# First layer's experts with tokens in rows: ScalarE applies the gates, GpSimd adds to the residual

## The chip, the cores and the metric

The kernel runs on one core of a Trainium2 chip. The metric is the device time of one execution in microseconds (us), lower is better. The core has five engines that run programs of their own and meet at semaphores: TensorE (PE; its weight loads are listed apart as PEld), VectorE (DVE), ScalarE (ACT), GpSimd (POOL) and SyncE (SP), which issues DMAs.

## The reference, cut to what matters

Two layers over 2048 tokens of width 128. Each has a mixing part (a selective scan in the first, attention in the second) and a part with experts. The change is in the experts of the first layer: a shared expert without a gate and eight gated ones, all of them computed for every token.

```python
def _L0_ffn_ref(x, shared_w1, shared_w2, experts_w1, experts_w2, gate_w):
    shared = jnp.einsum('td,dh->th', x_flat, shared_w1.T)
    shared = jnp.einsum('th,hd->td', jax.nn.silu(shared), shared_w2.T)
    gate_logits = x_flat @ gate_w.T
    top_k_gates, top_k_idx = jax.lax.top_k(gate_logits, TOP_K)
    top_k_gates = jax.nn.softmax(top_k_gates, axis=1)
    gates = gates.at[jnp.arange(T)[:, None], top_k_idx].set(top_k_gates)
    h = jnp.einsum('td,ehd->teh', x_flat, experts_w1)
    expert_out = jnp.einsum('teh,edh->ted', jax.nn.silu(h), experts_w2)
    selected = jnp.einsum('ted,te->td', expert_out, gates)
    return (shared + selected).reshape(B, S, D)
...
x = x + _L0_attn_ref(_layernorm(x, axis=-1), ...)
x = x + _L0_ffn_ref(_layernorm(x, axis=-1), ...)
```

Width 128, hidden width 512, eight experts, the two best are used.

## The kernel before

The tokens are cut into four chunks of 512 (`tc` 0 to 3). Every engine's program is written out in one shared order (`scan_order`): 64 steps `k` of the scan, 16 for each chunk. A step has a fixed sequence of calls, and a call does something only on the engines that define it. In step k DVE runs two halves of `scanP` (L1411), `mulW` (L1417) and `scanX` (L1425); POOL runs `mulB(k+1)` (L1876), `mulC(k)` (L1883) and `clamp(k+2)` (L1892); PE ends the step with `sums(k-1)` (L669); ACT opens it with two Exp (L1160), for step k+2. `mulB(k+1)` writes a ring of three buffers and waits for `sums(k-2)`; `mulW(k+1)` waits for `mulB(k+1)`.

Between these calls lie slots in which a generator is pulled: three slots of a step for the prolog of the next chunk, four for the epilog, gates and experts (`ffn`) of the chunk before. So the experts of chunk tc run beside the scan of chunk tc+1, one expert per step; those of chunk 3 run after the scan, beside the first parts of the second layer, and then begin the next part.

`ffn(tc)` has 36 pulls n, four for each of nine experts x (x = 0 is the shared one). In pull n PE multiplies by a quarter of the first weight ("up", L725) into bank 4 or 5; ACT applies Silu (L1187) and writes one of six buffers HB; two pulls later PE multiplies this by a quarter of the second weight ("down", L716), and four downs are summed in one bank. For chunks 0 to 2 there is only one bank for downs, 6: the first down of expert x+1 waits for the semaphore `gated`, which says that expert x has been read out. For chunk 3 two banks alternate. In pulls of one step, PE's order is: up, down; up, down; up; up, down, down; then the sums. The first down of the next expert is the one right behind the fourth up.

The result of the downs has features in rows (partitions) and tokens in columns. The gates have tokens in rows, so PE transposes them (L700), ACT copies them out (L1179), SP writes them to DRAM and reads each expert's row back to all partitions (buffers GB). DVE multiplies bank 6 by GB into GO (L1506), POOL adds GO to FO (L1904), and at the end PE transposes FO back ("fold", L739) and DVE adds it to the residual x_tok (L1520). Of the shared expert, ACT makes a plain copy into FO (L1191). While ACT computes Silu and Exp in turn, each change loads a table (ACT_TABLE_LOAD).

Of the kernel before, what the change touches and what calls it, by code (L numbers as in the profile page):

```python
# [384 lines left out]
def build(nc, A, out):  # L385
    with ExitStack() as ctx:
# [47 lines left out]
        with ExitStack() as ph:  # L434
# [37 lines left out]
            gT0 = sa("gT0", [8, C])  # L472
            gd = nc.dram_tensor("gd", [4, 8, C], F32, kind="Internal").ap()
            GB = [sa(f"GB{i}", [128, C])[:, :] for i in range(3)]
# [117 lines left out]
        def tensor_program(e):  # L592
# [79 lines left out]
            def epilog(tc):  # L672
# [3 lines left out]
                w.wait_ge(S("x_ffn"), tc)  # L676
# [19 lines left out]
            def gates(tc):  # L696
                yield from idle(9)
                w.wait_ge(S("gt"), 18 * tc + 18)
                for b in range(4):
                    t = e.transpose(bank(SUM_BANK[tc])[0:8, 128 * b:128 * b + 128], G[:, b, :], ident[:, :])  # L700
                t.then_inc(S("mm_gT"), 1)
                yield
                yield from idle(2)

            def down(i):

                tc, n = divmod(i, 36)
                w.wait_ge(S("hid"), i + 1)
                if n % 4 == 0:
                    if tc < 3:  # L710
                        w.wait_ge(S("gated"), 9 * tc + n // 4)
                    else:
                        w.wait_ge(S("gated"), 27 + max(n // 4 - 1, 0))
                        w.wait_ge(S("y"), 8)
                    w.wait_ge(S("g_row"), tc + 1)
                e.matmul(down_bank(tc, n // 4), f_w2[:, n // 4, n % 4, :], HB1[i % 6], start=(n % 4 == 0),  # L716
                         stop=(n % 4 == 3)).then_inc(S("mm_down"), 1)

            def ffn(tc):
# [14 lines left out]
                yield  # L734
                yield
# [5 lines left out]
                yield  # L741
                yield from idle(2)
# [78 lines left out]
            def qside(c):  # L821
# [4 lines left out]
                if c == 3:  # L826
                    w.wait_ge(S("x_ffn"), 4)
# [15 lines left out]
            def take_max(m):  # L843
                if m >= 2:
                    w.wait_ge(*freed(m - 2))
                else:
                    w.wait_ge(S("hid"), 144)
                    w.wait_ge(S("x_ffn"), 4)
# [489 lines left out]
        def vector_program(e):  # L1338
# [170 lines left out]
            def ffn(tc):  # L1509
                for n in range(36):  # L1510
                    if n % 4 == 2 and n >= 10:
                        gate_expert(tc, n // 4 - 1)
# [826 lines left out]
```

## Time and profile before

| | before |
|---|---|
| time, median of 3 runs | 1585.73 us (1584.5 to 1588.5) |
| profiled execution: own time, span | 1584.67 us, 1582.9 us |
| PE, DVE, ACT, POOL busy, share of the span | 83%, 79%, 66%, 42% |
| mean granted clock of TensorE | 0.906 of full speed |

A busy share is a mean over stages that have different limits. The scan takes up to about 625 us of the span, the experts of chunk 3 with the preparation of attention up to about 770 us, and attention and the second layer's experts the rest. The experts of the first layer run from 221 to 317 us, from 375 to 471 us, from 524 to 616 us, and from 643 to 767 us.

### The profile page before, as it was taken

To read this page: it belongs to the slowest core of one execution; us is meant where nothing else is said; L and a number is where in the kernel's file an instruction comes from. 1 tells how busy PE (TensorE), PEld (TensorE's weight loads), DVE (VectorE), ACT (ScalarE), POOL (GpSimd) and SP (SyncE) were. 2 spreads that over 40 slices of the span, in tenths; PEclk is the share of its full clock that TensorE was granted. 3 is DMA by queue.
4 is the path that set the end of the run, shared out by engine and by line. 5 is a ranking of instruction groups with operands and counts; after the bars stand their busy time and mean duration, and the time that the engine had idled before them with its cause. 6 is when DMAs were issued, how large, how long until landed. Compare 5 with 4: busy or idle time off the path is not lost.

```text
span 1582.9 us, 22572 instructions
## 1 busy us (share of the span) xinstructions
PE 1315.4 (83%) x8408; PEld 510.9 (32%) x8408; DVE 1250.9 (79%) x1499; ACT 1043.0 (66%) x1823; POOL 664.2 (42%) x609
## 2 busy tenths in 40 slices
PE   4355669966994797788749999999999999999998
PEld 1111233423342343333212222222222222225973
DVE  1889977888789888277579999999999999942522
ACT  3442357636862673545319999899989998998653
POOL 0678856875787586656232111311121114111440
PEclk9675589978997798899768999999999999999999
DMA  7122212312222220242121211000010000000210
GB/s 223 59 63 79 67 50 79 87 60 69 71 72 64 74 80 27 53 88 43 36 42 32 68 31 47 13 12 2 2 22 2 2 2 15 9 22 16 72 32 27
DMA packets 63696, 75.71 MB, mean 48 GB/s; under 512 B 8633, under 2 KB 39226, under 8 KB 63458
## 3 DMA queue, kind: packets, MB, share of 16 engines
q1 hardware_dynamic: 62818, 72.70, 17.0%
q0 software_dynamic: 768, 1.57, 0.3%
q8 instruction: 66, 1.08, 0.3%
q14 instruction: 44, 0.36, 0.1%
HBM read 66.04 MB, written 8.21 MB: 47 GB/s over the span
## 4 chain that ended last, share of the span: by engine, by line
PE 47%; DVE 29%; POOL 10%; issue 9%; ACT 4%; DMA 1%; SPq 1%; DVEq 0%; POOLq 0%; ACTq 0%
DVE mx L1636 15%; PE PS L945 11%; PE PS L933 6%; PE PS L716 4%; PE PS L902 4%; PE PS L725 4%; POOL D L1876 4%; DVE D L1425 3%; DVE PS L1411 3%; POOL D L1883 2%; PE PS L1017 2%; PE PS L1032 2%; PE PS L669 2%; DVE PS L1417 2%; PE PS L637 2%
## 5 line engine op out<-in xcount | busy, mean ns | idle before, releaser
L1297 ACT ACTIVATE aa<-PS 128x512 f32<-128x512 f32 x1024 | 551.6, 598 | 57.4 <-PE PS L933 46.6
L1636 DVE TENSOR_REDUCE mx<-PS 128x2 f32<-128x1024 f32 x480 | 552.2, 1216 | 8.0 <-PE PS L902 5.2
L945 PE MATMUL PS<-aa,D 128*32 128x256 f32 x4096 | 321.6, 391 | 1.5 <-ACT aa L1297 0.6
L933 PE MATMUL PS<-D 54*128 54x512 bf16 x1024 | 212.0, 390 | 9.3 <-ACT aa L1297 8.9
L669 PE MATMUL PS<-D,ident 128*128 128x512 f32 x256 | 157.5, 750 | 62.0 <-POOL D L1883 54.5
L902 PE MATMUL PS<-D 51*128 51x512 bf16 x960 | 189.9, 385 | 17.6 <-DVE mx L1636 17.0
L1990 POOL CAST n<-nm 4x512 bf16<-4x512 f32 x15 | 9.1, 604 | 445.9 <-ACT nm L1279 445.9
L1883 POOL TENSOR_TENSOR D<-D 128x1024 f32<-128x1024 f32 x64 | 150.8, 2356 | 72.6 <-DVE D L1425 72.6
L1160 ACT ACTIVATE D<-D,Am 128x512 f32<-128x512 f32 x128 | 85.1, 713 | 129.3 <-DVE D L1425 127.4
L1876 POOL TENSOR_TENSOR D<-D 128x1024 f32<-128x1024 f32 x64 | 150.5, 2352 | 41.1 <-PE PS L669 36.5
L1411 DVE TENSOR_TENSOR_SCAN PS<-PS,D 128x512 f32<-128x512 f32 x128 | 157.6, 1231 | 11.4 <-POOL D L1892 3.5
L725 PE MATMUL PS<-xnT,f_w 128*128 128x512 f32 x288 | 152.9, 631 | 6.0 <-ACT HB L1187 6.0
L1187 ACT ACTIVATE HB<-PS 128x512 f32<-128x512 f32 x144 | 85.1, 597 | 108.1 <-PE PS L725 107.7
L716 PE MATMUL PS<-HB,f_w 128*128 128x512 f32 x288 | 149.3, 626 | 0.9 <-ACT FO L1191 0.9
L945 PEld LDWEIGHTS PS<-aa,D 128*32 128x32 f32 x4096 | 84.2, 108 | 191.9 <-issue 153.0
L933 PEld LDWEIGHTS PS<-D 54*128 54x128 bf16 x1024 | 53.3, 93 | 219.6 <-ACT aa L1297 159.7
L1425 DVE TENSOR_TENSOR_SCAN D<-D,hl,PS 128x512 f32<-128x512 f32 x96 | 122.4, 1275 | 1.9
L669 PEld LDWEIGHTS PS<-D,ident 128*128 128x128 f32 x256 | 57.4, 237 | 145.0 <-POOL D L1883 73.5
L1417 DVE SCALAR_TENSOR_TENSOR PS<-PS,D 128x512 f32<-128x512 f32 x128 | 88.9, 694 | 3.5 <-POOL D L1876 0.5
L716 PEld LDWEIGHTS PS<-HB,f_w 128*128 128x128 f32 x288 | 57.2, 200 | 77.9 <-issue 70.5
L725 PEld LDWEIGHTS PS<-xnT,f_w 128*128 128x128 f32 x288 | 54.7, 200 | 72.7 <-issue 60.1
L598 PE MATMUL PS<-ident,xn 128*128 128x128 f32 x48 | 10.5, 358 | 79.8 <-ACT xn L1076 79.8
(323 smaller groups left out, 1634.4 us busy)
## 6 DMA issues: line engine op xcount, KB each, us to landing
D<-bc SPq DMA_DIRECT2D x128, 256.0 KB, 3.4
GB<-gd SPq DMA_DIRECT2D x32, 256.0 KB, 3.9
D<-sc SPq DMA_DIRECT2D x72, 64.0 KB
aa<-in_L_ffn_W SPq DMA_DIRECT2D x9, 256.0 KB, 3.2
D<-in_L_ffn_W SPq DMA_DIRECT2D x9, 256.0 KB, 3.7
f_w<-in_L_ffn_experts_w SPq DMA_DIRECT2D x1, 2048.0 KB, 9.6
f_w<-in_L_ffn_experts_w SPq DMA_DIRECT2D x8, 256.0 KB, 6.1
aa<-gh SPq DMA_DIRECT2D x1, 2048.0 KB, 9.3
```

Source lines behind the costliest of these rows:

```text
L669: e.matmul(bank(g), ident[:, :], wb[k % 3][:, g, :], start=(n == 0), stop=(n == 15)).then_inc(S("mm_sum"), 1)
L716: e.matmul(down_bank(tc, n // 4), f_w2[:, n // 4, n % 4, :], HB1[i % 6], start=(n % 4 == 0), stop=(n % 4 == 3)).then_inc(S("mm_down"), 1)
L725: e.matmul(bank(4 + i % 2), f_w1[:, n // 4, 128 * (n % 4):128 * (n % 4) + 128], XN[:, ts], start=True, stop=True).then_inc(S("mm_up"), 1)
L902: t = e.matmul(to[:, hh, :], query(hh, qc % 2, p, b), KS[64 * hh:64 * hh + 51, p, 512 * c:512 * c + 512], start=True, stop=True)
L933: e.matmul(take_exp(s + hh), KS[64 * hh:64 * hh + 54, p, 128 * kb:128 * kb + 128], QP[64 * hh:64 * hh + 54, qc % 2, p, :], start=True, sto ...
L945: t = e.matmul(PS[32 * j:32 * j + 32, 7, cs], va[:, kb, 9 * h:9 * h + 32], Pt[K % 3][:, 512 * j + 256 * n:512 * j + 256 * n + 256], start= ...
L1297: e.activation(Pt[K % 3][:, c:c + 512], bank((s + hh) % 3), ACT.Exp).then_inc(S("e_free"), 1)
L1411: e.tensor_tensor_scan(out=bank(3), data0=bank(2), data1=ab[k % 3][:, g, :], initial=0.0, op0=ALU.max, op1=ALU.mult).then_inc(S("sP"), 1)
L1425: e.tensor_tensor_scan(out=pb[k % 2][:, g, :], data0=ab[k % 3][:, g, :], data1=bank(3), initial=hl[:, 16 * g + n:16 * g + n + 1] if tc els ...
L1636: e.tensor_reduce(mx4[:, G % 2, b, 2 * pair:2 * pair + 2, c:c + 1], max_banks(m), AX.X, ALU.max).then_inc(freed(m)[0], 1)
L1876: e.tensor_tensor(wb[k % 3], DU[tc % 2][:, :, :], Bb[k % 3].unsqueeze(1).to_broadcast([128, 2, C]), ALU.mult).then_inc(S("wB"), 1)
L1883: e.tensor_tensor(wb[k % 3], pb[k % 2], Cb[k % 3].unsqueeze(1).to_broadcast([128, 2, C]), ALU.mult).then_inc(S("xC"), 1)
```

## The change

The operands of the down matmuls change places: four matmuls of 128x128 with a block of HB as the weight and the expert's second weight as the moving operand give a result with tokens in rows. Then a gate is one number per partition. ACT applies it as the scale of a Copy from the bank into GO, four pieces of 128 columns for each gated expert, one plain Copy of 512 columns for the shared one. POOL adds GO straight to x_tok, now for nine experts instead of eight, two slots after the Copy. The gates' transposes and copy, the DMAs through DRAM, DVE's multiplication, PE's fold and DVE's last addition go, and FO and GB with them.

```diff
-                w.wait_ge(S("x_ffn"), tc)
+                w.wait_ge(S("gated"), 9 * tc)
...
-            def gates(tc):
-                yield from idle(9)
-                w.wait_ge(S("gt"), 18 * tc + 18)
-                for b in range(4):
-                    t = e.transpose(bank(SUM_BANK[tc])[0:8, 128 * b:128 * b + 128], G[:, b, :], ident[:, :])
-                t.then_inc(S("mm_gT"), 1)
...
+            def down(i):
+
+                tc, n = divmod(i, 36)
+                x, j = divmod(n, 4)
+                w.wait_ge(S("hid"), i + 1)
+                if j == 0:
+                    if tc < 3:
+                        w.wait_ge(S("gated"), 9 * tc + x)
+                    else:
+                        w.wait_ge(S("gated"), 27 + max(x - 1, 0))
+                        w.wait_ge(S("y"), 8)
+                    w.wait_ge(S("logit"), tc + 1)
                 for b in range(4):
...
-                e.matmul(down_bank(tc, n // 4), f_w2[:, n // 4, n % 4, :], HB1[i % 6], start=(n % 4 == 0),
-                         stop=(n % 4 == 3)).then_inc(S("mm_down"), 1)
+                    t = e.matmul(down_bank(tc, x)[:, 128 * b:128 * b + 128], HB1[i % 6][:, 128 * b:128 * b + 128],
+                                 f_w2[:, x, j, :], start=(j == 0 and b == 0), stop=(j == 3 and b == 3))
+                t.then_inc(S("mm_down"), 1)
...
-                w.wait_ge(S("gated"), 9 * tc + 9)
-                w.wait_ge(S("ffn_sum"), 8 * tc + 8)
-                for b in range(4):
-                    t = e.transpose(bank(SUM_BANK[tc])[:, 128 * b:128 * b + 128], FO[:, 128 * b:128 * b + 128], ident[:, :])
-                t.then_inc(S("mm_fold"), 1)
...
+            def gate_expert(tc, x):
+
+                w.wait_ge(S("mm_down"), 36 * tc + 4 * x + 4)
+                w.wait_ge(S("ffn_sum"), 9 * tc + x - 1)
+                if x == 0:
+                    e.activation(GO[0], down_bank(tc, 0), ACT.Copy).then_inc(S("gated"), 1)
+                    return
+                w.wait_ge(S("gt"), 18 * tc + 18)
+                for b in range(4):
+                    t = e.activation(GO[x % 2][:, 128 * b:128 * b + 128], down_bank(tc, x)[:, 128 * b:128 * b + 128],
+                                     ACT.Copy, scale=G[:, b, x - 1:x])
+                t.then_inc(S("gated"), 1)
...
                     e.activation(HB1[i % 6], bank(4 + i % 2), ACT.Silu).then_inc(S("hid"), 1)
-                    if n == 6:
...
+                    if n % 4 == 2 and n >= 6:
+                        gate_expert(tc, n // 4 - 1)
                     yield
...
-                e.scalar_tensor_tensor(out=GO[x % 2], in0=down_bank(tc, x), scalar=1.0, in1=GB[n % 3], op0=ALU.mult,
-                                       op1=ALU.mult).then_inc(S("gated"), 1)
...
-                w.wait_ge(S("mm_fold"), tc + 1)
-                e.tensor_tensor(xs, xs, bank(SUM_BANK[tc]), ALU.add).then_inc(S("x_ffn"), 1)
...
-                    e.tensor_tensor(FO[:, :], FO[:, :], GO[x % 2], ALU.add).then_inc(S("ffn_sum"), 1)
+                    w.wait_ge(S("e_xn"), 4 * tc + 4)
+                    w.wait_ge(S("ffn_sum"), 9 * tc + x)
+                    e.tensor_tensor(xs_, xs_, GO[x % 2], ALU.add).then_inc(S("ffn_sum"), 1)
...
-                    if n % 4 == 2 and n >= 10:
-                        add(n // 4 - 1)
+                    if n % 4 == 0 and n >= 8:
+                        add(n // 4 - 2)
```

What the change does to the order is seen at three places. The first is ACT in one step of the experts of chunk 2, where no prolog runs beside them. Before, a step's Silu follow one another:

```order
L1160 ACT_TABLE_LOAD
L1160 ACTIVATE D<-D,Am 128x512 [waits sX]
L1160 ACTIVATE D<-D,Am 128x512
L1187 ACT_TABLE_LOAD [waits mm_down]
L1187 ACTIVATE HB<-PS 128x512 [waits mm_up]
L1187 ACTIVATE HB<-PS 128x512 [waits mm_down,mm_up] x3
```

Now the four pieces of the gated copy (L1171) stand between the third and the fourth Silu, which is L1180:

```order
L1143 ACT_TABLE_LOAD
L1143 ACTIVATE D<-D,Am 128x512 [waits sX]
L1143 ACTIVATE D<-D,Am 128x512
L1180 ACT_TABLE_LOAD
L1180 ACTIVATE HB<-PS 128x512 [waits mm_up] x2
L1180 ACTIVATE HB<-PS 128x512 [waits mm_down,mm_up]
L1171 ACTIVATE GO<-PS,G 128x128 [waits ffn_sum,mm_down]
L1171 ACTIVATE GO<-PS,G 128x128 x3
L1180 ACTIVATE HB<-PS 128x512 [waits mm_up]
```

The copy of an expert has moved behind the Silu that takes the third up of the next expert.

The second place is PE in the same chunk, from the third up of a step to its end. Before:

```order
L725 MATMUL PS<-xnT,f_w 128x512 [waits hid] x2
L716 MATMUL PS<-HB,f_w 128x512 [waits gated]
L716 MATMUL PS<-HB,f_w 128x512
L669 MATMUL PS<-D,ident 128x512 [waits xC]
L669 MATMUL PS<-D,ident 128x512
```

Now, with up on L716, down on L706 and the sums on L666:

```order
L716 MATMUL PS<-xnT,f_w 128x512 [waits hid] x2
L706 MATMUL PS<-f_w,HB 128x128 [waits gated]
L706 MATMUL PS<-f_w,HB 128x128 x7
L666 MATMUL PS<-D,ident 128x512 [waits xC]
L666 MATMUL PS<-D,ident 128x512
```

The place of the wait for `gated` is the same, one up behind the third; two matmuls have become eight, and the engine that is waited for is another.

The third place is DVE in the last two steps of the scan, where the experts of chunk 2 end. Before:

```order
L1411 SCALAR_TENSOR_TENSOR PS<-PS,D 128x512 [waits sX]
L1506 SCALAR_TENSOR_TENSOR GO<-PS,GB 128x512 [waits ffn_sum,d_G2,mm_down]
L1417 SCALAR_TENSOR_TENSOR PS<-PS,D 128x512 [waits sP]
L1425 SCALAR_TENSOR_TENSOR D<-D,hl,PS 128x512 [waits mW]
L1520 TENSOR_TENSOR x_tok<-x_tok,PS 128x512 [waits mm_fold]
L1411 SCALAR_TENSOR_TENSOR PS<-PS,D 128x512 [waits sX,clamp]
L1417 SCALAR_TENSOR_TENSOR PS<-PS,D 128x512 [waits wB,sP]
```

Now, with L1404, L1410 and L1418 for these three operations of the scan:

```order
L1404 SCALAR_TENSOR_TENSOR PS<-PS,D 128x512 [waits sX]
L1410 SCALAR_TENSOR_TENSOR PS<-PS,D 128x512 [waits sP]
L1418 SCALAR_TENSOR_TENSOR D<-D,hl,PS 128x512 [waits mW]
L1404 SCALAR_TENSOR_TENSOR PS<-PS,D 128x512 [waits sX,clamp]
L1410 SCALAR_TENSOR_TENSOR PS<-PS,D 128x512 [waits wB,sP]
```

Both operations that waited for PE's work on the experts are gone from DVE, here and in the other chunks.

## Rows read from the trace of the kernel before

**Rows 1.** Waits by engine, 560 to 612 us: total us, times, longest us

```profile
DVE GO L1506 <- PE PS L716: 7.9, 6, 1.3
```

**Rows 2.** Stretches: length, busy of PE, PEld, DVE, ACT, POOL, clock, DMA

```profile
261.40:313.50 52.10, 52.10 (x122) 22.85 (x121) 45.69 (x49) 38.81 (x52) 44.16 (x31) 1.00 0.26 71
541.40:602.80 61.40, 61.08 (x146) 26.98 (x145) 46.73 (x47) 45.67 (x62) 47.56 (x27) 1.00 0.30 88
641.00:765.00 124.00, 106.79 (x267) 43.02 (x266) 71.78 (x105) 63.50 (x87) 70.89 (x62) 0.93 0.30 58
```

**Rows 3.** The chain that ended last, 596 to 642 us: start, length, what

```profile
605.19 1.42 issue
...
606.64 1.27 POOL FO L1904
```

**Rows 4.** Timeline of one step of chunk 2's experts: start, length, idle before

```profile
571.34 1.88 PE L725 MATMUL PS<-xnT,f_w 128*128 128x512 f32 x4
...
571.54 0.69 DVE L1506 SCALAR_TENSOR_TENSOR GO<-PS,GB 128x512 f32<-128x512 f32 x1 [1.32 <-PE PS L716]
...
572.40 0.60 ACT L1187 ACTIVATE HB<-PS 128x512 f32<-128x512 f32 x1 [1.12 <-PE PS L725]
...
573.05 1.88 PE L716 MATMUL PS<-HB,f_w 128*128 128x512 f32 x4
...
579.92 1.88 PE L725 MATMUL PS<-xnT,f_w 128*128 128x512 f32 x4
```

**Rows 5.** Timeline of the shared expert's copy in chunk 2

```profile
544.56 1.88 PE L725 MATMUL PS<-xnT,f_w 128*128 128x512 f32 x4
...
545.62 0.60 ACT L1187 ACTIVATE HB<-PS 128x512 f32<-128x512 f32 x1 [0.82 <-PE PS L725]
546.12 0.59 ACT L1191 ACTIVATE FO<-PS 128x512 f32<-128x512 f32 x1
...
546.76 1.98 PE L716 MATMUL PS<-HB,f_w 128*128 128x512 f32 x4 [0.32 <-ACT FO L1191]
```

**Rows 6.** Timeline of the second layer's experts, matmuls and copies in pieces of 128

```profile
1515.02 1.06 PE L1017 MATMUL PS<-D 128*128 128x128 f32 x8
...
1515.91 1.06 PE L1032 MATMUL PS<-D 128*128 128x128 f32 x8
1516.11 1.14 ACT L1323 ACTIVATE D<-PS,D 128x128 f32<-128x128 f32 x4 [0.64 <-PE PS L1017]
```

**Rows 7.** Timeline of the normalisation in chunk 2, four pieces of 128 on ACT

```profile
542.68 1.64 ACT L1076 ACTIVATE xn<-x_tok,shift,rstd 128x128 f32<-128x128 f32 x4
```

**Rows 8.** Timeline of the end of chunk 2's experts and of the scan

```profile
610.82 1.88 PE L716 MATMUL PS<-HB,f_w 128*128 128x512 f32 x4
...
611.42 2.34 POOL L1876 TENSOR_TENSOR D<-D 128x1024 f32<-128x1024 f32 x1
612.74 0.69 DVE L1506 SCALAR_TENSOR_TENSOR GO<-PS,GB 128x512 f32<-128x512 f32 x1 [0.34 <-PE PS L716]
...
615.13 0.63 PE L739 MATMUL PS<-ident,FO 128*128 128x128 f32 x4 [2.43 <-POOL FO L1904]
...
615.79 0.69 DVE L1520 TENSOR_TENSOR x_tok<-x_tok,PS 128x512 f32<-128x512 f32 x1 [0.45 <-PE PS L739]
...
617.66 0.70 DVE L1417 SCALAR_TENSOR_TENSOR PS<-PS,D 128x512 f32<-128x512 f32 x1
...
621.71 1.28 DVE L1425 TENSOR_TENSOR_SCAN D<-D,hl,PS 128x512 f32<-128x512 f32 x1
```

**Rows 9.** Timeline around the second expert of chunk 0

```profile
254.38 1.08 ACT L1187 ACTIVATE HB<-PS 128x512 f32<-128x512 f32 x2
...
255.03 1.33 PE L725 MATMUL PS<-xnT,f_w 128*128 128x512 f32 x2 [2.44 <-ACT HB L1187]
...
256.15 3.41 PE L716 MATMUL PS<-HB,f_w 128*128 128x512 f32 x4
```

**Rows 10.** Timeline of the last part: a wait of PE for ACT

```profile
665.66 1.96 PE L800 MATMUL PS<-D,t2w 128*128 128x512 f32 x4 [1.15 <-ACT D L1262]
```

More of the change, by code:

```diff
@@ L733, in ffn @@
                 down(36 * tc + 35)
[L734 to L742 removed]
+                yield from idle(5)
             def later(tc):
@@ L905, in maxima @@
                 slot["max", m % 2] = m
-            scan_order(IDLE | dict(start=start, prolog=prolog, sums=sums, epilog=epilog, gates=gates, ffn=ffn, later=later,
+            scan_order(IDLE | dict(start=start, prolog=prolog, sums=sums, epilog=epilog, ffn=ffn, later=later,
                                    combine=combine, kside=kside, qside=qside, early=early, first=first,
@@ L1187, in ffn @@
                     e.activation(HB1[i % 6], bank(4 + i % 2), ACT.Silu).then_inc(S("hid"), 1)
-                    if n == 6:
-                        w.wait_ge(S("mm_down"), 36 * tc + 4)
-                        w.wait_ge(S("mm_fold"), tc)
-                        e.activation(FO[:, :], down_bank(tc, 0), ACT.Copy).then_inc(S("gated"), 1)
+                    if n % 4 == 2 and n >= 6:
+                        gate_expert(tc, n // 4 - 1)
                     yield
-                yield from idle(5)
+                yield
+                gate_expert(tc, 8)
+                yield from idle(4)
             def later(tc):
@@ L2131, in rows @@
                 e.dma_start(Cb[k % 3], bc[tc, 16 + n, :].partition_broadcast(128)).then_inc(S(f"d_C{k % 3}"), 16)
-            def gates(tc):
-                yield from idle(11)
-                w.wait_ge(S("g_row"), tc + 1)
-                e.dma_start(gd[tc], gT0[:, :]).then_inc(S("d_gd"), 16)
-                yield
-            def ffn(tc):
-                def gate_row(x):
-                    n = 8 * tc + x - 1
-                    w.wait_ge(S("d_gd"), 16 * (tc + 1))
-                    if x <= 3:
-                        w.wait_ge(S("gated"), 9 * tc)
-                    else:
-                        w.wait_ge(S("gated"), 9 * tc + x - 2)
-                    e.dma_start(GB[n % 3], gd[tc, x - 1, :].partition_broadcast(128)).then_inc(S(f"d_G{n % 3}"), 16)
-                for n in range(36):
-                    if n == 4:
-                        gate_row(1)
-                        gate_row(2)
-                        gate_row(3)
-                    elif n in (12, 16, 20, 24, 28):
-                        gate_row(n // 4 + 1)
-                    yield
-                yield from idle(5)
             def load_q(qc):
@@ L2206, in qside @@
                 yield
-            scan_order(IDLE | dict(start=start, prolog=prolog, rows=rows, gates=gates, ffn=ffn, kside=kside, qside=qside))
+            scan_order(IDLE | dict(start=start, prolog=prolog, rows=rows, kside=kside, qside=qside))
             meet(e, w)
```

46 lines of the change are left out of this document (9 added, 37 removed).

## The prediction

> **What bounds the kernel now.** I read first the chain that ended last. In the steps in which a chunk's experts run beside the scan it goes mainly through POOL, with gaps named "issue" of about 1.4 us between `mulB` and the addition of GO [rows 3]. Read alone this says that POOL waits for DVE's gating, and that taking DVE's gating and its additions out of the way shortens each step. The waits of the same stretch say more: DVE's gating itself sat idle 7.9 us in six cases, up to 1.3 us each, until PE had done the downs [rows 1]. So I went on to PE. Over 52.1 us of chunk 0's experts PE is busy all 52.10, at full clock, and in chunk 2's 61.08 of 61.4 [rows 2]. A busy PE is partly modelled, so I check it by starts: the third ups of two steps begin at 571.34 and 579.92 [rows 4], 8.58 us apart. Four f32 records with 512 columns each take 573.05 - 571.34 = 1.71 us, a matmul of two records therefore 0.86. A step holds four ups, four downs and two sums, ten matmuls: 8.6 us. The step is PE's work and nothing else. Anything that makes PE wait there comes out at the end one to one; nothing that only frees DVE or POOL does.
>
> **The new wait.** PE's order is third up, fourth up, first down of the next expert, and that down needs the bank read out. Before, DVE reads it at 571.54, while PE works on the ups, and the down starts at 573.05 without delay [rows 4]. Now ACT does it, behind the Silu of the third up, which can't start before this up is done: 572.40 - 571.34 = 1.06 us after its start [rows 4]. How long from there is seen at the shared expert, where ACT already stands in this place: the copy starts 546.12 - 545.62 = 0.50 after the Silu, lasts 0.59, and PE's down starts 0.05 later, at 546.76 instead of at 544.56 + 1.71 = 546.27 [rows 5]. That is a wait of 0.49 (the profile reports 0.32 of it as idle, since the ends of matmuls are modelled). A gated copy is four pieces of 128 columns. The nearest row is L1323: four pieces from PSUM, each with one number per partition, here as bias, 1.14 us together [rows 6]. So PE waits 1.06 + 0.50 + 1.14 + 0.05 - 1.71 = 1.04 us. Bounds: the four can't be shorter than the one plain copy of 0.59 (wait 0.49), and with two such operands and an SBUF source they took 1.64 [rows 7] (wait 1.54). I take 1.04, since from L1323 the gated copy differs only in using the number as scale.
>
> ScalarE: Activation LUTs, "What ACT_TABLE_LOAD costs", in the Trainium skill, gives for an instruction with one pointer operand 186 + 93 ns and 0.833 ns for each column, with 93 ns of overlap; its estimate for four pieces is 1.27 us, the wait 1.17 and the whole sum 2.5 us more than below. The same page under "Rules for kernel authors" says that multiplying belongs on VectorE. The trace so far sides with it, 0.69 us on DVE against 1.14.
>
> How often: experts 1 to 7 are each followed by a first down. In chunk 2 all seven cases lie in the saturated stretch: 7.3 us. In chunks 0 and 1 six do: 6.2 each. For expert 1 there PE waits anyway, for the Silu of the prolog's disturbed step: ACT's pair ends at 255.46, PE goes on with downs at 256.15 [rows 9]; the copies would start at about 255.36, end at 256.50, and PE starts 0.4 late. Together 7.3 + 2 x 6.6 = 20.5 us. In chunk 3 the down banks alternate and the wait is for two experts back: nothing.
>
> **The downs.** Eight records with 128 columns took 1515.91 - 1515.02 = 0.89 us [rows 6] against 0.86: 0.03 more for each, 36 x 0.03 = 1.1 in each of three chunks, and some 0.7 of it in chunk 3, where PE is busy 106.8 of 124 us [rows 2]: 4.0 us.
>
> **Gates.** PE no longer waits for G and transposes it, but its fourth up needs the Silu of the second, and ACT does this behind the Exp of the gates, which waits for the same chain on DVE. I take nothing; at most it is four transposes for each chunk, 0.63 us as in L739 [rows 8], 2.5 in all. The DMAs through DRAM lay in no wait.
>
> **The ends of the chunks.** Here the change gives back. After a chunk's last downs the scan goes at DVE's pace, and DVE is held by the last gating (0.34 wait and 0.69) and by the addition to x_tok (0.45 and 0.69), 2.17 us [rows 8]. It gains more than that. Without waits for PE, DVE comes to the last step as early as `mulB` allows. That ends at 611.42 + 2.34 = 613.76 [rows 8], and from `mulW` to the last scan it then takes 621.71 + 1.28 - 617.66 = 5.33 us [rows 8], so to 619.1 instead of 622.99: 3.9 us. POOL is no obstacle. The addition of expert 8 now stands ahead of `mulC` and ends at 612.7 + 0.05 + 1.14 + 0.05 + 1.27 = 615.2, when `mulC` began before too. (1.27 is the addition [rows 3].) In chunks 0 and 1 the scan that follows is bound by DVE as well. I take 3.9 for each of three, -11.7; the lower bound is 2.17, -6.5.
>
> **Chunk 3.** The last gating grows by 1.14 - 0.69 = 0.45, the fold (0.63) and DVE's addition (0.69) go: -0.9. The pieces put 8 x 1.14 = 9.1 us on ACT, which is busy 63.5 of 124 [rows 2]. They lie beside PE's work except where ACT's next operation is waited for at once. I count one such place in eight, +1.1. Both: +0.2.
>
> The other moves cost nothing. POOL has nine additions instead of eight, but 44.2 of 52.1 us busy leave room [rows 2]. An addition ahead of `mulB` delays it by up to 1.27, and `mulW` of the step after needs `mulB` only at the next step. ACT comes to 38.8 + 6 x 1.14 = 45.6 in a stretch that then lasts 59 us. Were this cover gone, each addition would cost its 1.27.
>
> **Sum.** 20.5 + 4.0 - 11.7 + 0.2 = +13.0 us. The profiled execution took 1584.67 (span 1582.9 and 1.8 around it), 1.1 under the median of 1585.73. So its like would take 1597.7, and the median 1598.7.
>
> **Rivals.** 1. *Not slower: PE has slack after all.* The chain names POOL and DVE [rows 3], and PE's ends are modelled. If POOL's order bounded the steps, the new waits would fill PE's holes; the downs' 4.0 too; and the ends remain: -11.7 + 0.2 = -11.5, 1574. For it speaks the chain, against it the 8.58 us of starts that ten matmuls fill exactly. It decides from a wait under (11.5 - 4.0 - 0.8) / 19 = 0.35 us, less than the 0.49 that the shared expert already shows. 12 in 100.
>
> 2. *The clock falls.* After a wait of 2.44 us PE ran four records in 3.41 us instead of 1.88 [rows 9]. If each of 19 waits did this, it would add 19 x 1.5 = 29 us: 1628. Against it: after waits of 0.32 [rows 5] and 1.15 us [rows 10] four records took 1.98 and 1.96, at full clock. 7 in 100. TensorE: Matmul & The Clock Gate, "A second HAM failure mode: psum-queue depth-cycling", in the Trainium skill, tells of a kernel whose frequent short idles between groups made the clock go back and forth; that is this rival, and the rows with short waits don't show it.
>
> 3. *The gain at the ends is small and the copies are short,* or other mixes near zero: 4 in 100.
>
> **How the numbers follow.** My forecast has 77 in 100. Its range: the copies' bounds move 19 waits by -0.55 or +0.50, -10.5 or +9.5, so 1588.2 to 1608.2; the smaller gain at the ends would give 1603.9. I give 1588 to 1609, with about 80 in 100 in it. What a measurement of this kernel can tell from no change is some 0.3%, 4.8 us, so "same" is 1581.0 to 1590.5. Faster: 8 of rival 1 and 1 of the mixes, 0.09. Same: 3 of the forecast, 4 of rival 1, 1 of the mixes, 0.08. Slower: the rest, 0.83.
>
> **What the profile after would show.** In each step of chunks 0 to 2, PE idle before the first down, released by ACT's copy into GO, six or seven times a chunk with about 0.9 us as reported; starts of third ups 9.7 to 9.8 us apart instead of 8.58; four pieces in about 1.14 us; no new table load before them. The scan's last `scanX` comes about 3.9 us earlier after the last down than now (622.99 - 612.70 = 10.3 us, then 6.4). Granted clock stays 1.00. The forecast is wrong if steps still take 8.6 us, if the pieces take much under 0.6 or over 1.6 us, or if the mean clock falls in these stretches.

## The result, and the profile after

| | before | after |
|---|---|---|
| time, median of 5 runs, same chip | 1586.47 us (1584.5 to 1588.5) | 1598.81 us (1597.23 to 1602.86) |
| ratio, 95% interval | | 1.0084 [1.0073, 1.0094] |
| span of the profiled execution | 1582.9 us | 1596.5 us |

The changed kernel is 12.3 us slower; +13.0 was forecast. A second timing of the same two kernels gave 1600.8 us and 1.0098 [1.0083, 1.0112].

From the page of the kernel after: busy time of each engine, and the shares of the chain that ended last.

```profile
PE 1319.0 (83%) x9240; PEld 586.4 (37%) x9240; DVE 1229.0 (77%) x1463; ACT 1071.5 (67%) x1947; POOL 667.6 (42%) x613
...
PE 53%; DVE 26%; issue 8%; ACT 6%; POOL 5%; DMA 1%; SPq 1%; DVEq 0%; POOLq 0%; ACTq 0%
```

The busy shares say next to nothing about the 12 us: DVE has 2% less, ACT 1% more. Who waits for the gated copies says it. This is the answer for the line of the four pieces in the kernel after: durations (min/median/max), and who waited for it (us, times).

```profile
L1171 ACT ACTIVATE GO<-PS,G x128: 359/371/397, 256.6 to 779.4; 128x128 f32<-128x128 f32 x128
...
  PE PS L706: 16.3, 19
```

Nineteen waits of PE, at its down matmuls, which is the number that the prediction counted (7 + 6 + 6). One of them in full, from the timeline of a step of chunk 2 (start, length, idle before). In these fences up stands on L716, down on L706, the sums on L666, the gated copy on L1171. It answers to [rows 4]:

```profile
572.71 1.88 PE L716 MATMUL PS<-xnT,f_w 128*128 128x512 f32 x4
...
573.76 0.60 ACT L1180 ACTIVATE HB<-PS 128x512 f32<-128x512 f32 x1 [1.15 <-PE PS L716]
...
574.26 1.13 ACT L1171 ACTIVATE GO<-PS,G 128x128 f32<-128x128 f32 x4
...
575.45 2.05 PE L706 MATMUL PS<-f_w,HB 128*128 128x128 f32 x16 [0.86 <-ACT GO L1171]
...
577.34 1.88 PE L666 MATMUL PS<-D,ident 128*128 128x512 f32 x4
```

The third up starts at 572.71, the copies at 574.26, and they end at 575.39; the down could have started at 572.71 + 1.72 = 574.43 and starts at 575.45. That is 1.02 us (forecast 1.04), of which the profile reports 0.86. One more row shows the step's length, the third up before it:

```profile
562.85 1.88 PE L716 MATMUL PS<-xnT,f_w 128*128 128x512 f32 x4
```

572.71 - 562.85 = 9.86 us where 8.58 stood before. Besides 1.02 for the wait, 0.12 are four downs of 0.89 instead of 0.86, and 0.10 were not foreseen: the two downs behind the wait take 577.34 - 575.45 = 1.89 instead of 2 x 0.89 (0.04 is left, from rounding).

The windows of the experts of chunks 0, 1, 2 and 3 (length, busy of PE, PEld, DVE, ACT, POOL, clock) answer to [rows 2]:

```profile
262.91:330.63 67.72, 58.58 (x286) 37.53 (x285) 51.53 (x52) 47.45 (x83) 51.30 (x37) 0.99 0.16 48
420.13:487.85 67.72, 58.59 (x286) 37.53 (x285) 52.13 (x53) 48.00 (x84) 51.31 (x37) 0.98 0.17 48
562.85:628.30 65.45, 59.44 (x290) 37.83 (x289) 43.82 (x41) 45.37 (x78) 43.92 (x26) 1.00 0.15 45
654.80:779.00 124.20, 106.64 (x482) 64.04 (x482) 68.12 (x97) 70.29 (x116) 71.10 (x63) 0.95 0.23 42
```

PE, which had no gap in these stretches, is now busy 58.6 of 67.7 us. The clock stayed at its upper level. What came back at the end of chunk 2 answers to [rows 8]:

```profile
628.30 1.95 PE L706 MATMUL PS<-f_w,HB 128*128 128x128 f32 x16
...
628.62 2.35 POOL L1846 TENSOR_TENSOR D<-D 128x1024 f32<-128x1024 f32 x1 [4.07 <-PE PS L666]
...
631.07 0.70 DVE L1410 SCALAR_TENSOR_TENSOR PS<-PS,D 128x512 f32<-128x512 f32 x1 [3.19 <-POOL D L1846]
...
635.12 1.28 DVE L1418 TENSOR_TENSOR_SCAN D<-D,hl,PS 128x512 f32<-128x512 f32 x1
...
635.95 3.59 PE L666 MATMUL PS<-D,ident 128*128 128x512 f32 x4 [3.98 <-POOL D L1853]
```

The last scan ends at 636.40, 6.2 us after the downs (630.2); before it was 10.3. But the sums at 635.95 take 3.59 us instead of 1.88: PE had stood for 3.98 us, and the granted clock is 0.50 from 635.8 to 639.2, the lower of its two levels. Six matmuls of the preparation (L772) follow, and only then the last sums. Before, the last sums were themselves the slow ones, but no other matmul stood in their way. The last sums before (first line) and after (second line):

```profile
625.68 3.78 PE L669 MATMUL PS<-D,ident 128*128 128x512 f32 x4 [3.29 <-POOL D L1883]
...
641.95 1.88 PE L666 MATMUL PS<-D,ident 128*128 128x512 f32 x4
```

They start 2.69 us behind the end of the last scan before (622.99) and 5.55 us behind it after; with their own lengths, 1.0 us of the gain is lost there.

**A ledger.** `mulB` runs once in each of the scan's 64 steps in both kernels, so its start after minus its start before tells where time goes. In the profiled executions it stands at +0.99 when the first experts begin, +9.22 at the end of chunk 0's experts, +5.32 once that end is past, +12.91 and +8.98 for chunk 1, and +17.20 at the end of chunk 2's experts, where the scan ends. From there other landmarks go on: +13.41 at the last scan, +14.43 at chunk 3's first transposes (L598 before, L595 after), +13.62 at the experts' last addition to x_tok, and +13.6 at the end of the span.

| | forecast | measured |
|---|---|---|
| ahead of the first experts | 0 | +1.0 |
| experts of chunks 0, 1, 2 (waits and downs) | 7.7 + 7.7 + 8.4 | 8.2 + 7.6 + 8.2 |
| ends of chunks 0, 1, 2 | 3 x -3.9 | -3.9, -3.9, -2.8 |
| chunk 3 and what follows | +0.9 | -0.8 |
| sum | +13.0 | +13.6 |

Chunk 2's growth is counted from +8.98. The +1.0 at the start lies where the two kernels run the same program. Over the other runs below it was between -0.2 and +1.8 us, so it is not the change's. The -0.8 lies in chunk 3's experts: from the first transposes to the last addition they take 127.07 us before and 126.26 after (126.25 in the second timing). What follows them took 815.45 us in one profile of the changed kernel and 818.67 in the other, with the same kernel, so differences of 3 us there are not the change's either.

### The profile page after: what moved, and what is told of

It is laid out like the page before. It is cut to its first block, busy times and chain, and to the rows that moved or that the text cites. A ratio compares the mean times of both kernels' runs of the same rounds, so it can differ in the third digit from the quotient of the medians.

```text
span 1596.5 us, 24193 instructions
## 1 busy us (share of the span) xinstructions
PE 1319.0 (83%) x9240; PEld 586.4 (37%) x9240; DVE 1229.0 (77%) x1463; ACT 1071.5 (67%) x1947; POOL 667.6 (42%) x613
## 4 chain that ended last, share of the span: by engine, by line
PE 53%; DVE 26%; issue 8%; ACT 6%; POOL 5%; DMA 1%; SPq 1%; DVEq 0%; POOLq 0%; ACTq 0%
DVE mx L1606 14%; PE PS L928 11%; PE PS L706 7%; PE PS L916 6%; PE PS L716 5%; PE PS L885 4%; PE PS L666 4%; DVE D L1418 3%; PE PS L1000 2%; PE PS L1015 2%; POOL D L1846 2%; DVE PS L1404 2%; PE PS L1036 2%; PE PS L1024 2%; PE PS L634 2%
## 5 line engine op out<-in xcount | busy, mean ns | idle before, releaser
L666 PE MATMUL PS<-D,ident 128*128 128x512 f32 x256 | 156.5, 745 | 63.2 <-POOL D L1853 57.5
L706 PEld LDWEIGHTS PS<-f_w,HB 128*128 128x128 f32 x1152 | 149.8, 200 | 78.1 <-issue 39.6
L716 PE MATMUL PS<-xnT,f_w 128*128 128x512 f32 x288 | 153.4, 633 | 27.8 <-ACT HB L1180 27.8
L706 PE MATMUL PS<-f_w,HB 128*128 128x128 f32 x1152 | 154.0, 285 | 17.3 <-ACT GO L1171 16.3
L1404 DVE TENSOR_TENSOR_SCAN PS<-PS,D 128x512 f32<-128x512 f32 x128 | 157.6, 1231 | 13.7 <-POOL D L1862 5.1
L1180 ACT ACTIVATE HB<-PS 128x512 f32<-128x512 f32 x144 | 85.7, 601 | 106.9 <-PE PS L716 106.6
L1418 DVE TENSOR_TENSOR_SCAN D<-D,hl,PS 128x512 f32<-128x512 f32 x96 | 122.7, 1278 | 2.7
L1410 DVE SCALAR_TENSOR_TENSOR PS<-PS,D 128x512 f32<-128x512 f32 x128 | 89.0, 695 | 45.0 <-POOL D L1846 42.7
L666 PEld LDWEIGHTS PS<-D,ident 128*128 128x128 f32 x256 | 54.1, 233 | 130.8 <-POOL D L1853 77.0
L716 PEld LDWEIGHTS PS<-xnT,f_w 128*128 128x128 f32 x288 | 50.2, 199 | 72.4 <-ACT HB L1180 37.3
L595 PE MATMUL PS<-ident,xn 128*128 128x128 f32 x48 | 10.9, 369 | 79.0 <-ACT xn L1059 79.0
```

The costliest lines, as they stand in the source:

```text
L666: e.matmul(bank(g), ident[:, :], wb[k % 3][:, g, :], start=(n == 0), stop=(n == 15)).then_inc(S("mm_sum"), 1)
L706: t = e.matmul(down_bank(tc, x)[:, 128 * b:128 * b + 128], HB1[i % 6][:, 128 * b:128 * b + 128], f_w2[:, x, j, :], start=(j == 0 and b == ...
L716: e.matmul(bank(4 + i % 2), f_w1[:, n // 4, 128 * (n % 4):128 * (n % 4) + 128], XN[:, ts], start=True, stop=True).then_inc(S("mm_up"), 1)
L1404: e.tensor_tensor_scan(out=bank(3), data0=bank(2), data1=ab[k % 3][:, g, :], initial=0.0, op0=ALU.max, op1=ALU.mult).then_inc(S("sP"), 1)
L1418: e.tensor_tensor_scan(out=pb[k % 2][:, g, :], data0=ab[k % 3][:, g, :], data1=bank(3), initial=hl[:, 16 * g + n:16 * g + n + 1] if tc els ...
```

## The experiments

Times are to be compared as ratios to the kernel before, timed beside them. Beside experiments 3, 4 and 6 that kernel took 1593.2 us instead of 1586; the profiles of these four runs have 8.2 to 8.6 us more in the routing of the second layer, between 1334 and 1425 us, which the change doesn't touch.

**1. The copy ahead of the Silu.**

```diff
+                    if n % 4 == 2 and n >= 6:
+                        gate_expert(tc, n // 4 - 1)
                     w.wait_ge(S("mm_up"), i + 1)
                     w.wait_ge(S("mm_down"), i - 5)
                     e.activation(HB1[i % 6], bank(4 + i % 2), ACT.Silu).then_inc(S("hid"), 1)
-                    if n % 4 == 2 and n >= 6:
-                        gate_expert(tc, n // 4 - 1)
```

> The changed kernel, with ScalarE's gated copy (and the shared expert's) put ahead of the Silu of the third up instead of behind it. The copy's results are then there while TensorE is still at the third and fourth up. Theory of the prediction (TensorE has no slack in the experts, and its 16.3 us of waits for GO, 19 of them, are what the change costs): those waits go, the third ups stand about 8.8 us apart instead of 9.85, and the time falls from 1598.8 to between 1575 and 1582, below the kernel before as well (1586.5), since the shortened ends of the chunks stay. Rival 1 (GpSimd's and VectorE's chain of the scan sets the length of a step, and TensorE's wait only fills slack): the waits go and the steps stay at 9.85, so the time stays at 1597 to 1600. Rival 3 (ScalarE is late now, and the Silu behind the copy becomes the wait): TensorE waits for the Silu at its next down instead, 0.5 to 1 us a step, and the time is 1590 to 1599.

1576.12 us, 0.9945 [0.9932, 0.9957]: 22.7 us less than the changed kernel, and less than the kernel before. The timeline of chunk 2:

```profile
564.38 1.88 PE L716 MATMUL PS<-xnT,f_w 128*128 128x512 f32 x4
...
573.11 1.88 PE L716 MATMUL PS<-xnT,f_w 128*128 128x512 f32 x4
...
573.31 1.14 ACT L1171 ACTIVATE GO<-PS,G 128x128 f32<-128x128 f32 x4 [0.29 <-PE PS L706]
...
574.32 1.30 ACT L1182 ACTIVATE HB<-PS 128x512 f32<-128x512 f32 x2
...
574.83 1.95 PE L706 MATMUL PS<-f_w,HB 128*128 128x128 f32 x16
```

The same four pieces begin 0.20 us after the third up instead of 1.55, and no wait is left. Steps are 8.73 us. The theory of the prediction holds; rivals 1 and 3 had 1597 to 1600 and 1590 to 1599. `mulB` at the end of chunk 2 stands 22.6 us (21.7 in the repetition) lower than after the change, the starts set equal. Not all of this is the gated copies'. The edit also moves the shared expert's plain copy, for which PE waits in each of the three chunks in the changed kernel:

```profile
553.11 1.88 PE L716 MATMUL PS<-xnT,f_w 128*128 128x512 f32 x4
555.31 2.05 PE L706 MATMUL PS<-f_w,HB 128*128 128x128 f32 x16 [0.32 <-ACT GO L1167]
```

That is 0.48 us and the 0.10 behind it, 1.7 us for three, and the kernel before has this wait too [rows 5]. So the waits for the gated copies cost 20.0 to 20.9 us. In chunk 3, where no down waits at once for a copy, the new order is worth 1.7 us more (its experts take 124.6 us).

**2. A shorter copy.**

```diff
-                for b in range(4):
-                    t = e.activation(GO[x % 2][:, 128 * b:128 * b + 128], down_bank(tc, x)[:, 128 * b:128 * b + 128],
-                                     ACT.Copy, scale=G[:, b, x - 1:x])
+                t = e.activation(GO[x % 2], down_bank(tc, x), ACT.Copy)
```

> The changed kernel with one plain ScalarE copy of 512 columns in place of the four gated pieces of 128; the gates are left out of the computation, which shortens the copy from 1.13 us to 0.59. Theory of the prediction: TensorE's wait for GO falls by the same 0.54 us at each of the 19 full waits, 10 us in all, to about 1588.5 (1586 to 1591), and the third ups stand 9.3 us apart. Rival 1 (TensorE has slack): no change, 1597 to 1600. If each wait had a price of its own beside its length (a fall of the clock, a refill of TensorE), the gain would differ from 0.54 a step.

The gates are left out of the computation. 1586.67 us, 1.0005 [0.9996, 1.0014]: 12.1 less. Two third ups and the down between them:

```profile
564.43 1.88 PE L716 MATMUL PS<-xnT,f_w 128*128 128x512 f32 x4
566.63 2.05 PE L706 MATMUL PS<-f_w,HB 128*128 128x128 f32 x16 [0.32 <-ACT GO L1170]
...
573.74 1.88 PE L716 MATMUL PS<-xnT,f_w 128*128 128x512 f32 x4
```

9.31 us for a step, 0.54 less, as the copy is 0.54 shorter. Nineteen times that is 10.3. Chunk 3's experts take 124.84 us instead of 126.26, 1.4 less; together 11.7 of the 12.1.

**3. A longer copy.**

```diff
-                for b in range(4):
-                    t = e.activation(GO[x % 2][:, 128 * b:128 * b + 128], down_bank(tc, x)[:, 128 * b:128 * b + 128],
-                                     ACT.Copy, scale=G[:, b, x - 1:x])
+                for c in range(8):
+                    t = e.activation(GO[x % 2][:, 64 * c:64 * c + 64], down_bank(tc, x)[:, 64 * c:64 * c + 64],
+                                     ACT.Copy, scale=G[:, c // 2, x - 1:x])
```

> The changed kernel with the gated copy in eight pieces of 64 columns instead of four of 128, the same result. It makes the copy longer and changes nothing else: a dose on the other side of the plain copy (which shortened the wait by 0.54 us and the whole by 12.1). An ungated copy of 512 takes 0.59 us and a piece of 128 0.371, so 64 columns less are worth about 0.037 us; four pieces take 1.13, which is 0.25 for each after the first; so eight take an estimated 0.33 + 7 x 0.22 = 1.85, 0.72 more than four. Theory (each us of the copy is a us of TensorE's wait, 19 to 21 times): +13.7 to +15, 1612 to 1614, steps 10.5 to 10.6 apart. Rival 1 (slack): 1597 to 1600. If ScalarE itself became the bound (it is 72% busy in these stretches), more than 15.

1.0204 [1.0187, 1.0222] against 1.0084 to 1.0098: 1.1 to 1.2%, 17 to 19 us, more than forecast. Eight pieces took 1.74 us (0.61 more, not 0.72), and a step of chunk 2 is longer by just that, 10.46. So 19 x 0.61 = 11.6 is the dose, and something else came on top. Chunk 3's experts take 1.7 us more (127.99). `mulB` shows the rest: 2.4 us in one step at the start of chunk 0 and of chunk 1 each, and 1.3 us in two other places. In that step PE stands for 2.40 to 2.44 us for the prolog's Silu in all kernels. After the change (first fence), and with eight pieces (second):

```profile
413.68 1.85 PE L716 MATMUL PS<-xnT,f_w 128*128 128x512 f32 x2 [2.40 <-ACT HB L1180]
415.32 2.94 PE L706 MATMUL PS<-f_w,HB 128*128 128x128 f32 x16
418.10 1.88 PE L666 MATMUL PS<-D,ident 128*128 128x512 f32 x4
```

```profile
421.49 1.51 PE L716 MATMUL PS<-xnT,f_w 128*128 128x512 f32 x2 [2.40 <-ACT HB L1180]
423.61 3.78 PE L706 MATMUL PS<-f_w,HB 128*128 128x128 f32 x16 [0.61 <-ACT GO L1171]
427.19 2.75 PE L666 MATMUL PS<-D,ident 128*128 128x512 f32 x4
```

Behind 2.40 us of standing, matmuls run at the lower clock level for a while in both: the granted clock is 0.50 from 414.0 to 417.3 in the first and from 422.1 to 428.9 in the second. The longer stretch goes with a further wait of 0.61 inside it: all downs (3.78) and half of the sums (2.75 instead of 1.88) are slow. That the further wait is the cause is not shown. In experiment 8 PE waits 0.51 us in the same place, and the clock is back at 1.00 from 412.9, with no step 2.4 us longer:

```profile
408.20 1.13 PE L716 MATMUL PS<-xnT,f_w 128*128 128x512 f32 x2 [2.40 <-ACT HB L1182]
409.84 3.45 PE L706 MATMUL PS<-f_w,HB 128*128 128x128 f32 x16 [0.51 <-ACT GO L1171]
413.13 1.88 PE L666 MATMUL PS<-D,ident 128*128 128x512 f32 x4
```

Rival 2 of the prediction was no fiction, then; the clock does fall here, in two steps of the kernel where a long wait stands, and not in the nineteen.

**4. Work for VectorE.** Seven operations a chunk, waiting for nobody, their result unused:

```diff
+                    if n % 4 == 2 and n >= 10:
...
+                        e.scalar_tensor_tensor(out=FO[:, :], in0=starts[:, :], scalar=1.0, in1=starts[:, :], op0=ALU.mult,
+                                               op1=ALU.mult).then_inc(S("extra"), 1)
```

> The changed kernel with seven operations of 128x512 (SBUF to SBUF, 0.6 to 0.7 us each) added to VectorE in every chunk's experts, at the places where the kernel before had its gating, but waiting for nobody. They write a tile that nothing reads. Theory of the prediction (TensorE sets the length of a step, VectorE idles 2 to 3 us of each): no change, 1597 to 1601, steps still 9.85. Rival 1 (the chain of VectorE and GpSimd sets it): 28 times 0.6 to 0.7 longer, 17 to 20 us, of which 13 to 15 in the first three chunks: 1611 to 1619.

1.0090 [1.0072, 1.0108]: no change from the changed kernel. The row of the added work:

```profile
L1500 DVE SCALAR_TENSOR_TENSOR FO<-starts 128x512 f32<-128x512 f32 x28 | 31.7, 1131 | 0.0
```

VectorE is occupied for 31.7 us more, and the steps stayed at 9.85 us. 28 x 0.68 = 19.0 us of it are the work itself, as planned; the rest is waiting for GpSimd (last section). So VectorE has room in every step of the changed kernel, and what the chain says of it is not the bound. These steps are 1.3 us longer than those of the kernel before; that VectorE's gating costs nothing in steps of 8.7 us either is shown by experiment 5 beside experiment 1.

**5. The layout without ScalarE.** VectorE multiplies as it did before, in the new layout:

```diff
+                e.scalar_tensor_tensor(out=GO[x % 2].rearrange("p (b d) -> p b d", b=4), in0=down_bank(tc, x).rearrange("p (b d) -> p b d", b=4),
+                                       scalar=1.0, in1=G[:, :, x - 1:x].to_broadcast([128, 4, 128]), op0=ALU.mult, op1=ALU.mult).then_inc(S("gated"), 1)
```

> The changed kernel with VectorE in place of ScalarE for the multiplication by the gates: one operation of 512 columns with the gates broadcast along each 128 of them, at the place in VectorE's program where the kernel before had its own; tokens stay in rows, no gate rows, no folding. It tells the layout from the engine. Theory of the prediction: VectorE did this operation in 0.69 us in the kernel before while TensorE did not wait for it, so the 16.3 us of waits go, the downs keep their +4, and of the 11.7 gained at the ends of the chunks the folding's part stays (about 2 each, an estimate), VectorE's part goes: 1578 to 1586. Rival 1: the time stays at 1596 or above, or VectorE's added work (24 operations of 0.69) makes it longer. Rival 2 of this run (in-order VectorE now waits for TensorE at this operation, the scan behind it): VectorE idles 1.3 us a step as before, without a price as long as TensorE is the bound.

1583.67 us, 0.9988 [0.9979, 0.9997]. The waits for the copy are gone from the steps (8.72 us). This operation and the waits in chunk 2:

```profile
572.92 0.69 DVE L1491 SCALAR_TENSOR_TENSOR GO<-PS,G 128x512 f32<-128x512 f32 x1 [1.46 <-PE PS L706]
```

```profile
DVE GO L1491 <- PE PS L706: 9.2, 7, 1.5
```

A gate broadcast along 128 columns costs the same 0.69 as a row of gates [rows 4], so no gate rows were needed for VectorE either. It stands 9.2 us for PE and this costs nothing in the steps: 8.72 us with the gating on VectorE, 8.73 without it in experiment 1. So relieving VectorE inside the steps was worth nothing. By `mulB` the ends of chunks 0 and 1 gain 1.7 and 1.8 us on the kernel before here, instead of 3.9. VectorE still has the last gating in this version and no longer the wait for the folding and the addition behind it, so in these two chunks each is about half of the gain (at the end of chunk 2 0.8 of 2.8). The new layout by itself is thus about as fast as the kernel before, or a little faster; what made the change slow is where ScalarE's copy stands.

**6. VectorE's waits at the ends, put back,** once in the changed kernel and once in that of experiment 1:

```diff
+            def ffn(tc):
+                yield from idle(37)
+                w.wait_ge(S("gated"), 9 * tc + 9)
+                yield
+                yield
+                w.wait_ge(S("ffn_sum"), 9 * tc + 9)
...
```

> The changed kernel with VectorE made to wait at the end of each chunk's experts as before: at the slot of the last gating for the last gated copy, and at the slot of the former residual addition for GpSimd's last addition. It computes the same. It tests the term of -3.9 us an end (-11.7), which the prediction gave to VectorE being free of the gating and of the wait for the folding; the landmarks of the changed kernel's trace give -3.9, -4.0 and -2.8. Theory: the ends lengthen by 2.2 to 3.9 each, the whole by 7 to 11 us, 1606 to 1610, with VectorE's last scan of the chunk again 8 to 10 us behind the last down (6.2 now). Rival (the ends gained because TensorE's four transposes of the folding and the bank between are gone, not VectorE's waits): no change, 1597 to 1600.

> The same waits of VectorE, put into the version with the gated copy ahead of the Silu (1576.1 us), where the gated copies are not waited for by TensorE. Theory: as there, +7 to +11, so 1583 to 1587. If the ends' gain were a part of the catch-up after TensorE's waits (VectorE and GpSimd had run ahead while TensorE stood), it would be smaller here than in the changed kernel itself. Rival as there: no change, 1575 to 1577.

1.0138 [1.0117, 1.0160] against 1.0084 to 1.0098, and 1.0005 [0.9993, 1.0017] against 0.9930 to 0.9945: 0.4 to 0.5% and 0.6 to 0.75%, 6 to 9 and 10 to 12 us. By `mulB`, with the starts set equal, the first lost 3.2, 3.5 and 2.6 us at the three ends, 9.3 in all. The last scan of chunk 2 in the first of the two, where the downs end at 637.9:

```profile
646.74 1.28 DVE L1418 TENSOR_TENSOR_SCAN D<-D,hl,PS 128x512 f32<-128x512 f32 x1
```

It ends at 648.0, 10.1 us behind the downs, as in the kernel before (10.3). The gain at the ends is VectorE not waiting for the experts' end. The rival, that it was the transposes and their bank, is out.

**7. The downs in their old form,** again with both orders of ScalarE. The result in the bank is then transposed against the residual:

```diff
-                for b in range(4):
-                    t = e.matmul(down_bank(tc, x)[:, 128 * b:128 * b + 128], HB1[i % 6][:, 128 * b:128 * b + 128],
-                                 f_w2[:, x, j, :], start=(j == 0 and b == 0), stop=(j == 3 and b == 3))
+                t = e.matmul(down_bank(tc, x), f_w2[:, x, j, :], HB1[i % 6], start=(j == 0), stop=(j == 3))
```

> The changed kernel with the down matmuls in the form of before: one of 128x512 with the weights stationary, instead of four of 128 columns with the hidden rows stationary. The result in the bank is then transposed against the residual, so this changes what is computed; waits, copies and adds stay. Theory of the prediction (this term +4.0 us: 0.03 us for each of the downs, and the loads of weights): the time falls by 4, and by some 2 more as the downs behind a wait took 1.89 us instead of 1.79 for two, so 1592 to 1595. Rival (four short matmuls with their own weight loads are the cost of the change, and the wait is slack): it falls by 10 or more. Rival 1 (TensorE has slack in the experts): no change.

> The gated copy ahead of the Silu, and the downs in the form of before (128x512, four times fewer instructions). The result in the bank is then transposed against the residual, which changes what is computed. It tests the prediction's term of +4.0 us for the downs where TensorE waits for nobody in a step; in the run with the waits left in, it did not show in the whole (1599.4 against 1598.8), though the steps were 0.12 us shorter. Theory: steps 8.58 instead of 8.73, the same 0.14 in each of the some 7 steps of a chunk in which TensorE is the bound, so 3 us in the first three chunks and 4 in all: 1572 where the version it starts from has 1576. Rival (the term is covered elsewhere: where the clock is low, or where VectorE or ScalarE is waited for, a shorter down wins nothing): 0 to 1.5 us less.

1599.39 us, 1.0087 [1.0074, 1.0100], and 1575.78 us, 0.9928 [0.9913, 0.9943], where the versions with four short matmuls have 1.0084 to 1.0098 and 0.9930 beside it. No gain in the whole, twice. In the steps it is there:

```profile
564.61 1.88 PE L714 MATMUL PS<-xnT,f_w 128*128 128x512 f32 x4
...
573.19 1.88 PE L714 MATMUL PS<-xnT,f_w 128*128 128x512 f32 x4
```

8.58 instead of 8.73 in the second version. Over the three chunks `mulB` and the first transposes behind them give 1.5 us for the first pair and 1.8 and 2.6 for the second (against its two profiles), the starts set equal. In chunk 3, up to the last addition, the old form then lost 1.4 us against the new one in the first pair and 2.4 in the second. In the first pair this is one jump of 1.9 us by the second down of the shared expert, and from there on the old form wins 0.5 back, as shorter downs should. PE idles 18 of 125 us there, and no line of its list of waits differs by more than 1.0 us; what makes the jump stays open.

**8. How near ScalarE is.** Experiment 1 with eight pieces, beside repetitions of the two versions.

> The changed kernel once more, beside the next three on one chip, as their base. Expected: 1.0084 of the kernel before, as in its first timing (1.0073 to 1.0094); where the whole is some us longer or shorter than in the first timing, both kernels are.

> The version with the gated copy ahead of the Silu, once more beside the changed kernel on one chip. Expected: 0.9945 of the kernel before (0.9932 to 0.9957 in its first timing), 22 to 23 us below the changed kernel.

> The gated copy ahead of the Silu, and in eight pieces of 64 columns (1.74 us instead of 1.13, measured in the changed kernel, where it cost 18 us). The copy now starts some 1.6 us before the fourth up ends. Theory: the downs wait for the Silu behind the copy only where the copy and this Silu together outlast the third and fourth up (about 1.7 us); with 1.74 the third Silu comes 0.6 us later than with four pieces, which TensorE would feel by at most that: between 0 and 0.6 us a step, 0 to 12 us in all, and nearer to 0 if the downs of the third have 0.5 us to spare. Rival 3 (ScalarE is the next bound, right behind TensorE): all of 0.6 a step, 12 us or more.

1600.8 us, 1.0098 [1.0083, 1.0112]; 1576.01 us, 0.9930 [0.9918, 0.9943]; 1586.84 us, 0.9997 [0.9987, 1.0007]. The two versions are 24.8 us apart here. The longer copy costs 10.8 us even in the good place:

```profile
562.64 1.88 PE L716 MATMUL PS<-xnT,f_w 128*128 128x512 f32 x4
...
571.75 1.88 PE L716 MATMUL PS<-xnT,f_w 128*128 128x512 f32 x4
573.75 2.05 PE L706 MATMUL PS<-f_w,HB 128*128 128x128 f32 x16
```

The down starts 2.00 us after the third up instead of 1.72 and, having waited, takes 0.10 longer; a step has 9.11 us, 0.38 more. So of 0.61 us of longer copy 0.33 were free. The profile's rows report no idle time for this wait of 0.28; only the starts show it. It falls between theory (nearer 0) and rival 3 (12 or more), nearer to the rival: ScalarE's copy with its Silu is the next bound behind PE.

## Why the prediction was right

**PE bounds the steps: shown.** Lengthening, shortening and moving the copy moved the steps by just the change in PE's wait (1 to 3); loading VectorE changed nothing (4), and its gating costs nothing in the shorter steps either (5). The chain's POOL and "issue" [rows 3] were a companion of the bound and not the bound.

**The wait, 1.04 us nineteen times: right.** 1.02 us each, nineteen times, 19.4 us. Each also makes the next two downs 0.10 longer, which the sum did not have, 1.9 us. The whole term, with 2 x 0.4 for expert 1, was 20.5. Counted by starts it is 21.6, with 0.3 for expert 1; by `mulB` it cost 20.0 to 20.9 (1). The pieces took 1.13 to 1.14, as the second layer's row had it [rows 6]. The estimate from ScalarE: Activation LUTs, "What ACT_TABLE_LOAD costs", in the Trainium skill, was 0.13 too high (its figures give 1.26, where the prediction wrote 1.27); the measurement decides. The same page's advice to multiply on VectorE ("Rules for kernel authors") agrees with experiment 5 in this place, but experiment 1 is faster still with the same multiplication on ScalarE: here the order within ScalarE mattered more than its speed, which in the good order costs the steps nothing with four pieces and 0.38 us each with eight (8). No table was loaded for the copies.

**The exception of expert 1, 2 x 0.4: too much.** The down does start later, 1.52 and 1.64 us after PE goes on behind the prolog's wait, where 1.13 and 1.06 stood before. But in chunk 1 not for the copies: the four pieces are over at 415.14, while PE's two ups, at the lower clock level, last until 415.32 above. The downs behind them are faster in turn. From the first of these ups to the first up of the next step it is 6.34 and 6.14 us in chunks 0 and 1 instead of 6.09 twice, 0.3 in all and not 0.8.

**The downs, +4.0: mis-sized.** 0.03 us each is right in a step. In the three chunks 1.5 to 2.6 came out, not 3.3, and in the whole nothing that can be told from the noise (7). The prediction multiplied by all 36 downs of a chunk, though only some seven of nine experts run in a stretch in which PE sets the pace; this reason is argued and has no run of its own.

**The ends, -11.7: right in mechanism, 1 us too much.** -3.9, -3.9, -2.8; undoing it cost 9.3 (6). At chunk 2's end 3.8 us had come back by the last scan; 1.0 was lost behind it, where PE's slow sums and the preparation's matmuls now stand ahead of the last sums.

**Chunk 3, +0.2 with 0.7 for its downs: mis-sized by 1.7.** Up to the experts' last addition -0.8 was measured, in both profiles of the changed kernel (126.26 and 126.25 us against 127.07). The copies do cost time here, as was said: with a shorter one the stretch takes 124.84, with a longer one 127.99, with the moved one 124.6. So other parts gave back more than the 0.9 counted; which, no run separates. The rest of the program differs by 3 us between executions of one kernel, so the span can't tell.

**The sum: right in its two large terms, lucky in the small ones.** Expert 1, the downs, the ends, chunk 3 and the price behind a wait were each off by 0.5 to 2 us, in both directions. That the whole came within 1 us of the forecast is luck to that extent.

**Rival 2, the clock: out for the nineteen waits.** The windows have 0.98 to 1.00. The passage in TensorE: Matmul & The Clock Gate, "A second HAM failure mode: psum-queue depth-cycling", in the Trainium skill, tells of repeated short idles that keep the clock going up and down. Nineteen waits of 1.0 us, and of 1.6 us in experiment 3 (granted clock 1.00 in the steps with them), one in every 10 us, did not do this.

## What to carry to other kernels

An operation that is moved to another engine takes a place in that engine's order, and what stands ahead of it there may matter more than its duration: behind one Silu the copy cost 20 to 21 us in the first three chunks, ahead of it nothing that the steps show, and the version so ordered is the fastest that computes the reference (0.9930 to 0.9945 of the kernel before). Look for which engine's instructions fill a step exactly, by the starts of two equal instructions and the sum of what lies between, before you free another one; here VectorE could be occupied 31.7 us longer for nothing, in steps of 9.85 us. Work freed off the bound pays only where the bound changes, here at three ends of chunks, 3 to 4 us each.

## What the runs showed that I had not expected

- A wait costs more than itself: the two downs behind any of these waits, even of 0.28 us, took 1.88 to 1.89 us instead of 1.79. For ten waits that is another microsecond. PE's weight load had waited for the copy as well (in the step shown at first it starts at 575.45, with the down), so it could not be done ahead; that this is the 0.10 is likely and not tested.
- A wait of 0.28 us of PE (573.75 in experiment 8) is reported as no idle time, one of 1.02 as 0.86.
- A short wait after a long one can be dear: 0.61 us inside the slow phase behind 2.40 us of standing went with 2.4 us of lost time, in both chunks (0.99 us as reported in chunk 0); 0.51 us in the same place in experiment 8 did not.
- The added operation of experiment 4 has no operand in PSUM, and its mean of 1.13 us is a mixture. It took 0.68 us in the 11 of 28 cases in which GpSimd did nothing meanwhile. In 12 cases it met a GpSimd operation that ran already and took 0.92 to 2.59 us, which is each time what was left of the GpSimd operation and some 0.55; one such pair stands below. In 5 cases it stayed at 0.68 with GpSimd busy beside it; in one of them the GpSimd operation that began during it, `mulB`, took 2.62 us instead of 2.35. `mulW`, with an operand in PSUM, takes 0.68 to 0.70 whatever GpSimd does (512 columns, f32).

```profile
585.71 1.27 POOL L1886 TENSOR_TENSOR x_tok<-x_tok,GO 128x512 f32<-128x512 f32 x1 [0.17 <-ACT GO L1171]
...
586.13 1.40 DVE L1500 SCALAR_TENSOR_TENSOR FO<-starts 128x512 f32<-128x512 f32 x1
```

- Halving the columns of a piece on ScalarE made eight of them 1.74 us where four take 1.13: 0.20 against 0.25 for each after the first, so nearly all of a short piece is its fixed part.
